# VectorE's order in the second layer of a vision tower: score copy and residual ahead of the grid of a pair, maximum and difference behind it

## The reference

```python
h = h + _L0_attn_ref(_layernorm(h), ...)      # first layer: weights 1 + s + s*s/2
h = h + _L0_ffn_ref(_layernorm(h), ...)       # y = x_q @ w_q.T + bias, both rounded to a 4 bit grid
h = h + _L1_attn_ref(_layernorm(h), ...)      # second layer: softmax
h = h + _L1_ffn_ref(_layernorm(h), ...)       # low rank, with gelu

# in _L0_ffn_ref, for blocks of 32 features
amax = jnp.max(jnp.abs(xb), axis=-1, keepdims=True)
scale = exp2(floor(log2(amax)) - 2) * exp2(d)
xs = xb / scale
q = sign(xs) * _fp4_round(clip(abs(xs), 0.0, 6.0))

# in _L1_attn_ref, 16 heads of 16 features, causal
scores = jnp.einsum('bhqd,bhkd->bhqk', q, k) / math.sqrt(hd)
scores = jnp.where(causal[None, None], scores, -10000.0)
probs = jax.nn.softmax(scores, axis=-1)
ctx = jnp.einsum('bhqk,bhkd->bhqd', probs, v)
```

## Time and profile before

| | |
|---|---|
| median of 3 runs | 257.46 us (257.4 to 257.49) |
| the profiled execution | 258.99 us, span 257.3 us |
| TensorE busy | 238.8 us (93% of the span) |
| VectorE busy | 183.2 us (71%) |
| ScalarE busy | 144.1 us (56%) |
| GpSimd busy | 153.4 us (60%) |

### The profile page before, as it was taken

How to read it: one execution, slowest core, us unless ns; L and a number is a source line. 1 busy time by engine, 2 the same in 40 slices (tenths; PEclk the granted TensorE clock), 3 DMA queues, 4 the chain that set the end, 5 groups by cost and what they waited for, 6 DMA issues and landing times.

```text
span 257.3 us, 7730 instructions
## 1 busy us (share of the span) xinstructions
PE 238.8 (93%) x3077; PEld 187.0 (73%) x3077; DVE 183.2 (71%) x348; ACT 144.1 (56%) x322; POOL 153.4 (60%) x234
## 2 busy tenths in 40 slices
PE   6599999979999799999999998899999998989992
PEld 6488888858888687887887887688888885344331
DVE  0434968324679999999999999998768888377021
ACT  3122314287998677878746754574555556823640
POOL 6432888525966777795889749676656661155000
PEclk9999999999999999999999999999999999999998
DMA  5959942000000000000001010001101110001021
GB/s 149 242 135 248 302 103 65 0 0 4 3 3 3 0 3 3 3 0 4 4 20 36 25 40 29 20 30 40 35 28 34 33 35 33 3 0 54 19 75 48
DMA packets 12967, 12.26 MB, mean 48 GB/s; under 512 B 4464, under 2 KB 12356, under 8 KB 12932
## 3 DMA queue, kind: packets, MB, share of 16 engines
q1 hardware_dynamic: 12504, 11.76, 16.8%
q10 hardware_dynamic: 428, 0.01, 0.1%
HBM read 7.95 MB, written 1.25 MB: 36 GB/s over the span
## 4 chain that ended last, share of the span: by engine, by line
PE 61%; DVE 27%; issue 5%; DMA 3%; ACT 2%; SPq 0%; DVEq 0%; ACTq 0%
PE psum L1329 11%; PE psum L1398 9%; PE psum L1567 4%; DVE img L1092 4%; PE psum L1720 3%; DVE big L1084 3%; PE psum L1658 3%; DMA img<-in_x 3%; PE psum L1708 3%; PE psum L1552 3%; PE psum L1444 3%; DVE st L1039 3%; PE psum L1307 2%; PE psum L1632 2%; PE psum L1484 2%
## 5 line engine op out<-in xcount | busy, mean ns | idle before, releaser
L1398 PE MATMUL psum<-hnT,a 128*128 128x114 f32 (+1 forms) x352 | 48.5, 281 | 0.2 <-ACT mT L740 0.2
L1398 PEld LDWEIGHTS psum<-hnT,a 128*128 128x128 f32 x352 | 43.3, 191 | 4.8 <-issue 1.5
L486 POOL TENSOR_SCALAR big<-mT,parmask 128x228 f32<-128x228 f32 x22 | 22.8, 1048 | 19.8 <-ACT mT L710 19.8
L491 POOL TENSOR_SCALAR ve<-mvs 114x1 f32<-114x1 f32 x44 | 16.9, 384 | 28.0 <-DVE mvs L1041 25.8
L1329 PE MATMUL psum<-wT,patchT 128*114 128x256 f32 (+1 forms) x132 | 30.1, 381 | 0.4 <-ACT patchT L645 0.4
L492 POOL TENSOR_TENSOR rstd<-ve,nhalf 114x1 f32<-114x1 f32 x44 | 27.1, 615 | 3.7
L519 POOL TENSOR_TENSOR big<-big,img 114x912 f32<-114x912 f32 (+1 forms) x11 | 21.8, 1984 | 11.2 <-ACT big L775 11.0
L1329 PEld LDWEIGHTS psum<-wT,patchT 128*114 128x114 f32 (+1 forms) x132 | 22.5, 175 | 5.6 <-issue 0.9
L1084 DVE SCALAR_TENSOR_TENSOR big<-big,img 114x912 f32<-114x912 f32 (+1 forms) x11 | 16.5, 1498 | 8.9 <-ACT big L764 8.9
L764 ACT ACTIVATE big<-psum 114x912 f32<-114x912 f32 (+1 forms) x22 | 18.8, 906 | 6.0 <-PE psum L1444 5.8
L1039 DVE BATCH_NORM_STATS2 st<-h_all 114x6 f32<-114x256 f32 x44 | 18.8, 428 | 1.5
(11 more groups left out here) (169 smaller groups left out, 557.9 us busy)
## 6 DMA issues: line engine op xcount, KB each, us to landing
img<-in_x SPq DMA_DIRECT2D x6, 576.0 KB, 9.8
img<-v_tok SPq DMA_DIRECT2D x66, 38.0 KB
out<-h_all SPq DMA_DIRECT2D x10, 114.0 KB
w_raw<-in_L_tok_W SPq DMA_DIRECT2D x3, 256.0 KB, 7.8
a_raw<-in_L_attn_Wq SPq DMA_DIRECT2D x1, 256.0 KB, 6.8
a_raw<-in_L_attn_Wk SPq DMA_DIRECT2D x1, 256.0 KB, 7.0
a_raw<-in_L_attn_Wv SPq DMA_DIRECT2D x1, 256.0 KB, 7.2
a_raw<-in_L_attn_Wo SPq DMA_DIRECT2D x1, 256.0 KB, 9.9
```

The lines of the kernel that those rows point to most:

```text
L486: nc.gpsimd.tensor_scalar(mX[:, :, o, :], mT[:, :, :], parmask[:, o:o + 1], None, ALU.mult).then_inc(L["mX"], 1)
L1398: return nc.tensor.matmul(bk[:, m * T:m * T + TW[t]], w[:, c, m * 128:(m + 1) * 128], hnT[:, c, 0:TW[t]], start=(c == 0), stop=(c == DC - 1))
```

## The change

`keep(t)` is cut in two: `keep` is only the copy under the mask now, and `below_maximum(t)` holds the maximum and the difference. In most iterations the second follows the first as before. In iterations 2 and 4 (tiles 3 and 5) VectorE takes the copy, the residual (in iteration 4 also ffn_residual(9)), then the grid of pair 4 or 5, and only then maximum and difference. The grid stood at the end of the iteration before. `quantised` stands behind `spread` and not ahead of it. On GpSimd the rounding of the pair moves from iterations 1 and 3 to 2 and 4, behind `expand`.

```diff
 GpSimd, attention()
                     if t + 2 < NT:
                         expand(L, t + 2)
+                    if t in (2, 4):
+                        round_to_grid(NP - 2 if t == 2 else NP - 1)
...
-                    if t == 1:
-                        round_to_grid(NP - 2)
                     if t == 3:
                         rstd_f_step(NT - 3)
-                        round_to_grid(NP - 1)

 VectorE, attention()
                     if t + 1 < NT:
                         keep(t + 1)
+                        if t not in (2, 4):
+                            below_maximum(t + 1)
...
-                    if t == 2:
-                        quantised(NP - 2)
                     if 3 <= t <= 5:
                         ffn_residual(NT - 6 + t)
-                    if t == 4:
-                        quantised(NP - 1)
+                    if t in (2, 4):
+                        grid(NP - 2 if t == 2 else NP - 1)
+                        below_maximum(t + 1)
                     if t + 1 < NT:
                         spread(t + 1)
+                    if t in (2, 4):
+                        quantised(NP - 2 if t == 2 else NP - 1)
                     if t == 0:
                         scales(NP - 2)
-                    if t == 1:
-                        grid(NP - 2)
                     if t == 2:
                         scales(NP - 1)
-                    if t == 3:
-                        grid(NP - 1)
```

More of the change, by code:

```diff
@@ L1152, in keep, with below_maximum @@
                     take_pairs(0, 2, 4)
+            def below_maximum(t):
+                L = lay[1]
                 dve.wait_ge(L["masked"], t + 1)
@@ L1192, in layer0 @@
                         keep(0)
+                        below_maximum(0)
                     divide(t)
```

## The result

| | before | after |
|---|---|---|
| median | 257.43 us (4 runs, 257.31 to 257.49) | 267.62 us (4 runs, 265.82 to 268.66) |
| ratio | | 1.0386 (95%: 1.0356 to 1.0417) |
| profiled execution | 258.99 us, span 257.3 | 266.98 us, span 265.2 |
| mean granted clock of TensorE in that one | 0.996 | 0.974 |

The changed kernel is 10.2 us slower, where 4.0 us had been forecast and 263.8 us was the upper end of the range. Its runs lie 2.8 us apart, those of the kernel before 0.2 us.

The account below looks back on a forecast made before the run. The prediction took TensorE and VectorE, taking turns, to bound the kernel. Iteration 2 cost 1.6 us and iteration 4 2.4, in sum 4.0 on 257.46: 261.4 us, range 260.0 to 263.8 for 8 in 10.

Parts of the forecast that it names:

- The late operand: Iterations 2 and 4: the later difference delays ScalarE's exponential and oT, making out_proj(2) 1.4 us and out_proj(4) 2.2 us late.
- The first part: Iteration 2: earlier copy and residual remove TensorE's two waits, 2.16 us; it stands ready for out_proj(2) at 162.0, not 164.17.
- VectorE beside GpSimd: Stretching by shared work: grid beside expand 0.3 us in iteration 2 and 0.2 in iteration 4, difference beside rounding 0.6.
- Rival (b): Grids wait for both expand instructions: 1.4 us more at iteration 2, 1.5 at iteration 4, 264.3 us; chance 0.15.
- VectorE's queue ahead of keep(4): Iteration 2: spread(3), quantised(4) and scales(5) make keep(4) 1.65 us late and the turned weights of tile 3 1.6 late.
- Rival (c): TensorE's clock falls to 1.2 GHz behind its idle time ahead of out_proj(2), doubling 2.5 us of work: 263.9 us; chance 0.05.
- (a): Both places: oT comes in time, so TensorE's 2.16 us come back, 255.3 us; chance 0.03.
- (d): Iteration 2 gives its 2.16 us and iteration 4 costs 2.2, so they cancel at 257.5 us; chance 0.03.

Follow-up runs that it names:

- the filling: Changed kernel with 26 idle transposes on TensorE ahead of out_proj(2) and 16 ahead of out_proj(4): 261.30 us, ratio 1.0144.
- iteration 4 alone: Changed kernel with the old order back in iteration 2, so only iteration 4 changed: 263.03, 262.91, 259.77 and 259.73 us.
- the half filling: Changed kernel with 12 idle transposes on TensorE ahead of out_proj(2) and 8 ahead of out_proj(4): 262.76 us.
- five copies: Kernel before with five 128x512 copies of spare tiles on ScalarE ahead of take_oT(7): 264.07 us.
- three copies: Kernel before with three 128x512 copies of spare tiles on ScalarE ahead of take_oT(7): 258.73 us, ratio 1.0057.

## Why the prediction was wrong

**The late operand: right, in place and size.** In the times of the profile before (1.68 us later than those of after, by scores(3)), the copy was forecast at 157.3 and came at 157.33, weigh(3) at 163.75 and came at 163.57, out_proj(2) at 165.55 and came at 165.32. With the clock held by the filling, iteration 2 (scores(3) to the turned weights of tile 3) took 13.30 us against 11.88, 1.4 us more where 1.6 was forecast, and iteration 4 (scores(5) to out_proj(4)) 9.42 against 7.06, 2.4 as forecast. The whole cost 3.84 us where 4.0 was forecast: 261.3 us is the time of the changed kernel without the clock. The first part, that the two waits of TensorE go, is right and worth nothing, as said there.

**VectorE beside GpSimd: right in size.** The grid took 159.68 - 157.40 = 2.28 us beside expand(4), 0.28 more than without a clash (0.3 taken); in iteration 4 it was 1.67 for 1.40, 0.27 more (0.2 taken). The difference took 1.38 us and not 0.79, 0.59 more (0.6 taken). Rival (b) falls. The rule on the shared ports that the prediction weighed (the Trainium skill, "SBUF — State Buffer", "Who interferes with whom") would have made whichever of the two starts second wait for the whole of the other, and the prediction priced it as each grid behind both instructions of expand. The rows show neither: stretches of 0.14, 0.04 and 0.12 us on L960 to L962, while expand took 2.59 us for its two, 0.86 more than the 1.73 in the earlier trace rows, where no grid ran beside it, and less than the 1.59 us that L960 to L962 last. Here the measurement decides, for this pair of operations: GpSimd paid most.

**VectorE's queue ahead of keep(4): right, but hidden in the changed kernel.** There the scores at half clock came later still, and VectorE waited 1.99 us for them. With the clock held, keep(4) started without a wait, 1.4 us later than before (1.65 forecast; both counted from scores(3)), and the turned weights stood 1.00 us behind the start of the copy, with no wait of TensorE that the profile names:

```profile
166.62 0.86 DVE L1146 COPY_PREDICATED sm<-keep,psum 114x608 f32<-114x608 int32 x1
```

```profile
166.47 1.10 PE L1401 MATMUL psum<-hnT,a 128*128 128x114 f32 x8
167.62 0.97 PE L1635 MATMUL psum<-ident,img 114*128 114x114 f32 x8
```

**The clock: this step failed.** Rival (c) named it, with a wait of 3.5 us ahead of out_proj(2), which came as 3.30. It was wrong in three ways. It got a chance of 0.05. What spoke against it was one row, a wait of 2.33 us at the start of the program with the clock at 1.00 behind it; one case in which it did not fall was read as a rule. And its price was the 2.5 us of work right behind the wait, where the half clock held for 9.6 us of work and cost 4.5; the second place, where the forecast itself had a new wait of 2.4 us on an engine that had none, was not considered at all, and cost 1.7 us in the profiled run. The sum should have carried both, some 6 us, and the range should have reached to 268. The whole miss, 10.2 - 4.0 = 6.2 us, is this term.

**The other rivals.** The gain of (a) and the cancelling of (d) needed weigh(3) before 162.4; it came at 163.57.

## What to carry to other kernels

A wait of TensorE has two prices: its length, and, in most runs of the kernels here with waits near 2 us and more between dense stretches, the half clock behind it, here 4.6 us more for 2.0 us of wait (264.07 - 257.46 - 2.0). So a change that turns two waits of 1 us into one of 2 us can be a loss even though the sum is the same. When instructions are moved in one queue, look who waits for the one that is now late, and then what stands behind that waiter in its own queue: here one late difference held the two copies behind an exponential that nobody needed yet. (Taking take_oT ahead of the exponential on ScalarE is the obvious cure; no run here tried it.) If a wait of TensorE cannot be avoided, cheap matmuls into a free bank held the clock here where they left waits of 0.5 us, and in two runs of four did not where they left 2.0; a spread between runs of 0.2 us in place of 2.8 tells whether they do.

## What the runs showed of the hardware that was not expected

- Length alone does not decide whether the clock falls. It stayed at 1.00 behind waits of 0.97, 1.05, 1.11, 1.32 and 1.60 us in every profile; behind 1.99 to 2.23 us it fell in the profiled executions, but two of four runs with iteration 4 alone (2.20 us in the profile) and two of four with the half filling kept a clock of 0.997 to 1.000; behind 2.33 us at the start of the program it stayed. What tells these apart is open.
- How long the half clock holds differs too, though TensorE works without a pause behind each wait: 9.6 us of work behind the first wait of the changed kernel and 9.7 with five copies, 6.9 with iteration 4 alone, 3.4 behind the second wait of the changed kernel. So its price can't be read from the length of the wait.
- It need not begin inside the wait. Behind the first wait of the changed kernel it began 0.7 us before the end of the wait, with iteration 4 alone 0.8 us behind it, with five copies 1.7 us behind it.
- The kernel before has runs at 257.4 and some at 258.4 to 258.95 us. The profiled one took 258.99 us: TensorE waited 2.33 us for the first image copy there, and 0.70 us in the profile after. This is ahead of everything that the change touches, and is why stretches and not absolute times are compared above.
- A transpose of 128x128 took 0.11 us in the middle of the program and 0.23 us (3.67 us for 16) among the first of it, though the granted clock is given as 1.00 at both places. The first clock record of a trace stands at 5.9 us in the changed kernel and at 7.9 us in the run with three copies, and a stretch ahead of it reads 1.00 all the same. The pace of the transposes changes at just these times: ten of them that start behind it take 1.26 us in the changed kernel, and ten that start ahead of it 1.92 us in the run with three copies. So the 1.00 of the first 6 to 8 us is no measurement, and the halving of the pace is the same factor as at 0.50. The wait of 2.33 us at 7.5 us of the profile before lies behind its first record (6.1 us), and its 1.00 stands.

```profile
6.22 1.26 PE L1290 MATMUL psum<-ident 128*128 128x128 f32 x10
```

```profile
6.51 1.92 PE L1291 MATMUL psum<-ident 128*128 128x128 f32 x10
```
